# First stage of a fused attention and feed-forward layer: K and Q0 by halves of tokens, swapped on TensorE

## The reference

```
Q = x Wq^T + bq (32 heads of 16);  K, V = x Wk^T + bk, x Wv^T + bv (8 heads of 16)
Q, K = rope(Q, K)                  rope(a) = a * cos + rot_half(a) * sin
w = softmax(Q K^T / 4);  attn = w V;  y = LN(x + attn Wo^T + bo)
out = LN(y + ((silu(y Wg^T * gs) * (y Wu^T * us)) Wd^T) * ds)
```

## Time and profile before

| | us |
|---|---|
| median of 3 runs | 1176.72 |
| lowest and highest | 1174.79, 1180.6 |
| profiled execution, its own time | 1180.09 |
| its span in the trace | 1178.3 |
| mean granted TensorE clock | 0.961 of 2.4 GHz |

### The profile page before, as it was taken

The page is one execution under the profiler, slowest core; times in us unless marked ns, Lnnn a source line. Parts: engine busy times, 40 slices in busy tenths (PEclk is TensorE's granted clock), DMA queues, the critical chain, the costliest instruction groups (busy, mean ns, idle before and its releaser), DMA issues. The chain is left out here.

```text
span 1178.3 us, 14659 instructions
## 1 busy us (share of the span) xinstructions
PE 1091.8 (93%) x5634; PEld 543.7 (46%) x5634; DVE 786.6 (67%) x880; ACT 632.2 (54%) x1178; POOL 194.0 (16%) x158
## 2 busy tenths in 40 slices
PE   7799999999899999998999999999789899999995
PEld 4333333333333443333333333333336478888884
DVE  4488689996869768685569999999402345262534
ACT  1127688786668658682367878878453012222221
POOL 0290020000320011210003004980000100000002
PEclk9858999999899999999999999999799999999998
DMA  5862134127231413422015236511205020000000
GB/s 201 187 268 52 29 87 88 29 44 154 68 80 67 70 35 80 87 76 42 9 38 116 60 104 157 162 64 29 102 10 159 4 90 36 1 1 36 1 36 36
DMA packets 36139, 88.19 MB, mean 75 GB/s; under 512 B 12640, under 2 KB 12896, under 8 KB 33632
## 3 DMA queue, kind: packets, MB, share of 16 engines
q1 hardware_dynamic: 36064, 87.20, 28.3%
HBM read 49.43 MB, written 23.86 MB: 62 GB/s over the span
## 5 line engine op out<-in xcount | busy, mean ns | idle before, releaser
L342 DVE TENSOR_REDUCE nmx<-PSA 128x1 f32<-128x1024 f32 x512 | 600.0, 1216 | 125.4 <-PE PSA L331 125.2
L411 ACT ACTIVATE Bn<-PS 128x512 f32<-128x512 f32 x1024 | 530.2, 604 | 216.0 <-PE PS L405 215.7
L331 PE MATMUL PSA<-Kt,Qt 48*128 48x512 f32 x1024 | 411.9, 481 | 15.1 <-DVE nmx L342 9.6
L405 PE MATMUL PS<-Qt,Kt 50*128 50x512 f32 x1024 | 382.6, 455 | 40.0 <-ACT Bn L411 22.5
L405 PEld LDWEIGHTS PS<-Qt,Kt 50*128 50x128 f32 x1024 | 172.0, 188 | 342.9 <-ACT Bn L411 298.6
L424 PE MATMUL PV<-Bn 128*32 128x512 f32 x2048 | 280.1, 620 | 0.0
L331 PEld LDWEIGHTS PSA<-Kt,Qt 48*128 48x128 f32 x1024 | 174.3, 193 | 60.8 <-DVE nmx L342 41.4
L813 PE MATMUL PSA<-x1Th,wr 128*128 128x512 f32 x344 | 136.5, 397 | 0.5 <-DVE sg L833 0.5
L813 PE MATMUL PSA<-x1Tl,wr 128*128 128x512 f32 x344 | 135.2, 393 | 0.0
L833 DVE SCALAR_TENSOR_TENSOR sg<-PSA,us,sg 128x512 f32<-128x512 f32 x43 | 32.1, 748 | 137.4 <-ACT sg L824 137.2
L824 ACT ACTIVATE sg<-PSA,gs 128x512 f32<-128x512 f32 x43 | 29.5, 689 | 163.9 <-PE PSA L813 163.9
(11 more groups left out here) (84 smaller groups left out, 560.1 us busy)
## 6 DMA issues: line engine op xcount, KB each, us to landing
Qt<-pscr SPq DMA_DIRECT2D x96, 128.0 KB, 5.4
pscr<-A SPq DMA_DIRECT2D x20, 512.0 KB, 3.6
A<-in_wf SPq DMA_DIRECT2D x11, 768.0 KB, 7.0
wr<-A SPq DMA_DIRECT2D x33, 256.0 KB, 3.2
vscr<-Bn SPq DMA_DIRECT2D x32, 256.0 KB, 2.0
Kt<-pscr SPq DMA_DIRECT2D x96, 64.0 KB, 2.5
A<-A SPq DMA_DIRECT2D x20, 256.0 KB, 3.7
A<-in_xT SPq DMA_DIRECT2D x4, 1024.0 KB, 8.6
```

What stands on the lines that cost most here:

```text
L331: r = pe.do(lambda e, h=h, p=p: e.matmul(ps[:, h, :], Qt[i][p:p + NC_, g % 2, 128 * qt:128 * qt + 128], Kt[i][p:p + NC_, 512 * h:512 * h + ...
L342: r_mxs[hh, s] = dve.do(lambda e: e.tensor_reduce(nmx[:, hh % 2, c0:c0 + 1], ps, AX.XY, ALU.max, negate=True), c_rel[s])
L405: r = pe.do(lambda e: e.matmul(PS2[:, c % 3, :], Kt[i][rows, 128 * kt:128 * kt + 128], Qt[i][rows, g % 2, 512 * qh:512 * qh + 512], start= ...
L411: r_exp[c] = act.do(lambda e: e.activation(Pb[c % NP_], PS2[:, c % 3, :], ACT.Exp, scale=0.25), c_exp)
```

## The change

1. K and Q0 are made by halves of 512 tokens. The swap of the two 64-row halves is a matmul with a 128x128 permutation (`turn_pairs`), not two DMAs. POOL multiplies by cos, DVE by sin (straight from the PSUM bank), DVE adds. The parts go from SBUF straight into `Kt` and `Qt` of group 0 (`gather_k0`, `gather_q0`): 6 and 24 DMAs, of which ACT issues 2 and 6, and the first 16 maxima wait only for the first half of the queries. The way through DRAM stays for the later groups.
2. The products of V and Q1 are spread between the maxima: one V tile (four matmuls of 128 columns) or one Q1 matmul behind every second maximum. Their PSUM place is `PS2`. Q2 moves into unit (0,9), Q3 from (1,2) to (1,10). The copy of Q1 on ACT stands behind unit (0,2).
3. The loads of wo, bo, ds, gs, us go behind unit (0,0); x comes in eight pieces behind units (n,0) and (n,8) of groups 0 to 3. `add_bo(0)` goes behind (1,10), `add_bo(1)` behind (3,10).
4. Three float32 matmuls on constants stand ahead of K. ACT issues the loads of Wk, of the bias and of the permutation; the other loads have another order. `gather(2)` goes from (0,3) to (0,10).

```
+        def turn_pairs(i, h, bank, r_ev):
+            cols = slice(512 * h, 512 * h + 512)
+            raw, qrot, cos, sin = (x[:, cols] for x in (qraw[i], qrots[i], cosT, sinT))
+            pe.wait(r_ev, r_swap)
+            r_sw = pe.do(lambda e: e.matmul(bank, swap, raw, start=True, stop=True), c_swp)
+            pool.wait(r_ev, r_sw, r_cos)
+            r_c = pool.do(lambda e: e.tensor_tensor(raw, raw, cos, ALU.mult), c_cs)
+            dve.wait(r_sw, r_sin)
+            r_free = dve.do(lambda e: e.tensor_tensor(qrot, bank, sin, ALU.mult), c_rp)
+            dve.wait(r_free, r_c)
+            r = dve.do(lambda e: e.tensor_tensor(raw, raw, qrot, ALU.add), c_rp)
+            act.wait(r)
+            r_hi = act.do(lambda e: e.copy(qrot.bitcast(F32R), raw), c_hm)
+            dve.wait(r_hi)
+            r_lo = dve.do(lambda e: e.tensor_tensor(raw, raw, qrot, ALU.subtract), c_lo)
+            return r_hi, r_lo, r_free
...
+        def gather_q0(qh, r_hi, r_lo):
+            cols = slice(512 * qh, 512 * qh + 512)
+            for part, j, r in ((0, 0, r_hi), (0, 2, r_hi), (1, 1, r_lo)):
+                for g in range(4):
+                    q = act if qh == 0 and g >= 2 else sp
+                    q.wait(r)
+                    p = 64 * (g // 2) + 16 * j
+                    v = q.do(lambda e, p=p, g=g, part=part: e.dma_start(
+                        Qt[0][p:p + 16, g % 2, cols].bitcast(F32), (qrots, qraw)[part][1][g:128:8, cols]),
+                        c_rep0[qh], 16)
+            r_rep[0, qh] = v
...
-        first = [project(0, 4, True), project(0, 0, True)]
-        for k in range(3):
-            for g in first:
-                next(g, None)
-        gather(0)
-        r_vp[0] = values(0)
-        second, third = project(0, 1, False), project(0, 2, False, True)
-        next(second)
-        next(third)
-        gather(1)
-        load_late()
...
+        pe.wait(r_v1)
+        for _ in range(3):
+            pe.do(lambda e: e.matmul(PV[:, :], Vflat[:, 0:128], Vflat[:, 0:512], start=True, stop=True))
+        banks = [slot()[1], slot()[1]]
...
+        r_k = [fill(0, 0), fill(0, 1)]
+        r_part = [turn_pairs(0, h, PS2[:, h, :], r_k[h]) for h in range(2)]
+        r_q = [fill(1, 0)]
+        fill(1, 1, range(1))
+        gather_k0(*r_part[1][0:2])
+        r_part.append(turn_pairs(1, 0, PS2[:, 2, :], r_q[0]))
+        gather_q0(0, *r_part[2][0:2])
+        r_q.append(fill(1, 1, range(1, KT)))
+        r_part.append(turn_pairs(1, 1, PV[:, :], r_q[1]))
+        r_idle.append(r_part[3][2])
+        vals, second = values(0, True), project(0, 1, True)
+        next(vals)
+        gather_q0(1, *r_part[3][0:2])
...
+        fine = itertools.chain(vals, second)
+        for k in range(8):
+            advance(4)
+            next(fine, None)
+        for k in range(LEAD):
+            advance(4)
+            next(fine, None)
+        for _ in range(16 - 1 - 8 - LEAD):
+            next(fine, None)
+        put(0, 2, lambda: next(second, None))
+        put(0, 4, lambda: next(second, None))
+        put(0, 0, lambda: load_late("wo", "bo", "ds", "gs", "us"))
+        for part in range(4):
+            put(part // 2, 8 * (part % 2), lambda part=part: load_x(0, part))
+            put(2 + part // 2, 8 * (part % 2), lambda part=part: load_x(1, part))
+        put(1, 10, lambda: add_bo(0))
+        put(3, 10, lambda: add_bo(1))
+        spread(project(0, 2), 0, 9, (6, 2))
+        spread(project(0, 3), 1, 10, (6, 2))
```

More of the change, by code:

```diff
@@ L1 @@
+import itertools
 from contextlib import ExitStack
@@ L228, in post_ln_layer, with product, project @@
         r_idle = []
-        def project(b, m, fast, idle=False):
+        def product(ps, b, m, h, k, c):
+            pe.wait(r_wqk[m], r_xT[b][h])
+            last_xT[b] = pe.do(lambda e: e.matmul(ps, wqk[:, m, k, :], xT[:, h, k, :], start=(k == 0), stop=(k == KT - 1)),
+                               c)
+            return last_xT[b]
+        def project(b, m, idle=False):
             s, ps = (None, PS2[:, 0:2, :]) if idle else slot()
-            pe.wait(r_wqk[m])
+            if idle:
+                pe.wait(r_idle[-1])
             for h in range(2):
-                pe.wait(r_xT[b][h])
                 for k in range(KT):
[L237 to L240, removed]
-            last_xT[b] = r
+                    r = product(ps[:, h, :], b, m, h, k, c_fill if (h, k) == (1, KT - 1) else None)
+                    if idle and (h, k) != (1, KT - 1):
+                        yield
             i = qn[0] % 2
@@ L280, in values @@
                         start=(k == 0), stop=(k == KT - 1)), c_fill if last else None)
+                if idle and t < 7:
+                    yield
             last_xT[b] = r
@@ L287, in values @@
                     bv[:, :].rearrange("p (o v c) -> p o v c", o=1, v=NKV).to_broadcast([128, 4, NKV, HD]),
-                    ALU.add), c_v if h == 0 else c_rel[s])
-            return c_rel[s].now()
+                    ALU.add), c_v if idle or h == 0 else c_rel[s])
+            r_vp[b] = v
+            if idle:
+                r_idle.append(v)
+            yield
+        r_vp = {}
         c_mr = [count(f"c_mr{i}") for i in range(3)]
@@ L327, in maxima @@
             s, ps = slot()
-            pe.wait(r_rep[n])
+            pe.wait(r_rep[n, qt // 4])
             for h in range(2):
@@ L564, in put, with fill @@
             background.setdefault((n, w), []).append(f)
+        pe.wait(r_v1)
+        for _ in range(3):
+            pe.do(lambda e: e.matmul(PV[:, :], Vflat[:, 0:128], Vflat[:, 0:512], start=True, stop=True))
+        banks = [slot()[1], slot()[1]]
+        def fill(i, h, ks=range(KT)):
+            m = (4, 0)[i]
+            for k in ks:
+                r = product(banks[i][:, h, :], 0, m, h, k, c_fill if k == KT - 1 else None)
+            if ks[-1] < KT - 1:
+                return None
+            act.wait(r, r_bqk)
+            return act.do(lambda e: e.activation(qraw[i][:, 512 * h:512 * h + 512], banks[i][:, h, :], ACT.Identity,
+                                                 bias=bqk[:, m:m + 1]), c_ev if h == 0 else c_rel[i])
+        qn[0] = 2
+        r_k = [fill(0, 0), fill(0, 1)]
[11 more added lines that the diff above has]
+        gather_q0(1, *r_part[3][0:2])
+        for i, m in enumerate((4, 0)):
+            sp.wait(r_part[2 * i + 1][1])
+            write_parts(0, m, i)
+            free_raw[i] += (c_rep0[0].now(), c_rep0[1].now())
+        gather(1)
         stream = [(n, qt, g) for n in range(NG) for qh in range(2) for qt in range(4 * qh, 4 * qh + 4)
@@ L581, in advance @@
                 next(halves, None)
-        for k in range(16):
-            if k == 4:
-                next(second, None)
-            if k == 8:
-                next(third, None)
-            if k == 13:
-                next(second, None)
-            advance(2)
-        advance(4 * LEAD)
-        next(third, None)
-        add_bo(0)
-        add_bo(1)
-        spread(project(0, 3, False), 1, 2, (6, 2))
+        fine = itertools.chain(vals, second)
[17 more added lines that the diff above has]
+        spread(project(0, 3), 1, 10, (6, 2))
         def load_b1():
@@ L1076 @@
         "ident": np.eye(128, dtype=np.float32),
+        "swap": np.roll(np.eye(128, dtype=np.float32), 64, 0),
     }
```

84 lines of the change are left out of this document (53 added, 31 removed).

## The result

| | before | changed |
|---|---|---|
| median, us | 1175.76 (4 runs, 1173.67 to 1180.6) | 1190.07 (4 runs, 1188.18 to 1196.95) |
| ratio | | 1.0126, 95% interval 1.0074 to 1.0179 |
| profiled span, us | 1178.3 | 1189.3 |
| mean granted clock | 0.961 | 0.964 |

The medians differ by 14.3 us, the forecast said 8.2; 1190.07 lies inside the range of 1171 to 1199. The ratios leave out runs more than 1.5% above the fastest of the same kernel, so a ratio can differ from that of two medians.

The account below looks back on a forecast made before the run. TensorE, busy 93% of the span, was taken as the bound, so an added matmul costs its own time unless PE waits there. Terms -6.0 + 7.5 + 6.2 + 0.5 = +8.2 us gave 1184.9 from the median; range 1171 to 1199.

Parts of the forecast that it names:

- The first reduction: VectorE's first maxima reduction moves from 49.39 to about 34.9 us; sign: a start at 33 to 36 us.
- From there to the end of Q1: First reduction to Q1's product, 34.9 to 71 us: 12 pairs 29.4, V's evacuation 1.3, Q1 matmuls 3.4, low clock 2.
- From there to unit 3: Q1's product to unit 3's V matmuls takes 19.5 us, to 90.5; ACT's copy of Q1 waits 3 to 5.
- My price for having no such wait: At Q1's copy on ACT: with the rotation early enough, unit 3 would come 7 us better.
- Q2's block: Q2's projection, moved from the gap ahead of the maxima into unit 9, costs +7.5 us.
- The split: Split of group 1's maxima behind unit 11 waits for Q2's POOL rotation: +6.2 us with low clock, bounds 0 and 6.2.
- `add_bo(1)`: Behind unit 58 it meets the split behind unit 59: one or two instructions of 1.2 us, partly hidden, +0.5 us.
- The copies of Q2 and the sum on ACT: These copies on ACT come closer together: cost nothing, bound 1 us.
- The sum: First stage -6.0, Q2's block +7.5, split +6.2, `add_bo(1)` +0.5: whole kernel +8.2 us, chance 0.42.
- A: Rival, first stage: the clock holds as PE's gap shrinks under 2 us; about -1 us, 1175.7 us, chance 0.20.
- B: Rival: the split behind unit 11 misses POOL; +2.0 us, 1178.7 us, chance 0.22.
- C: Rival: low clock lasts through V and Q1; 12 pairs cost 17 us instead of 2; +24 us, 1201, chance 0.16.

Follow-up runs that it names:

- E5: Changed kernel with five more constant matmuls between Q0's last products and the swap of its second half; ratio 1.0064 to before, median 1189.67 us against 1180.35.
- E1: Changed kernel with Q1's copy on ScalarE behind unit (0,5) instead of (0,2), its write behind (0,7); ratio 1.0142 to before, median 1190.63 us.
- E3: Changed kernel with Q1's copy behind unit (0,5), its write behind (0,7), and Q2's products in unit (0,10); ratio 1.0112 to before, median 1189.31 us.
- E4: Kernel before with one part alone: Q2's products in unit (0,9) instead of ahead of the maxima; ratio 1.0134, median 1189.20 us against 1175.43.
- E2: Changed kernel with Q2's products in unit (0,10) instead of (0,9); ratio 1.0098 to before, median 1193.19 us over 10 runs.
- E9: Kernel before with Q2's products alone moved from the gap ahead of the maxima into unit (0,10); ratio 1.0124, median 13.2 us above before.
- E12: The changed kernel measured once more, unchanged, over 9 runs; ratio 1.0105 to before.
- E7: Changed kernel with five V tiles ahead of the last swap, three behind; Q1 and Q2 between maxima, Q1's copy ahead of scores; 1175.28 us against 1180.35, ratio 0.9961.

## Why the prediction was right, and where its sizes were off

**The first reduction: forecast 34.9, measured 38.13**, outside the 33 to 36 us that were named as its sign. The method was right, the low-clock steps and the issues were under-priced. The issues on ACT cost 0.66 us each, not the 0.46 read from SP: +1.2. It isn't a matter of the queue: four of K's DMAs held SP for 2.77 us, 0.69 each, so the row taken, six reads from DRAM, was no measure for copies from SBUF to SBUF. The swap at the low clock took 2.07 instead of 0.89 (+1.2), and the V tile behind it, at that clock too, held the maxima, for which the reduction waited 0.46 us. The prediction let the clock fall only in the phase after the gap and priced none of the gap's own successors with it. The blocked add was as forecast: 1.67 us instead of 0.69, and the sin product at 16.08, which reads PSUM, took 0.69 beside POOL. By the rule of the Trainium skill (SBUF — State Buffer, "SBUF: two separate sides") it should be so, and the trace agrees.

**From there to the end of Q1: forecast 36.1 us, measured 36.7** (38.13 to 74.87). Right in sum, and partly by luck: the clock was low for about 14 us (59 to 72.7) where I had put 4, and by E5, where it held, that cost 3.9 us and not 2. Most of the pairs ran at the high clock and cost nothing.

**From there to unit 3: forecast 19.5, measured 18.6** (74.87 to 93.50). POOL ended the rotation 12.7 us after Q1's product, exactly as forecast. ACT came to the copy later, since the units ahead of it ran slowly too, so it waited 2.64 us, less than the 3 to 5 named as the sign. My price for having no such wait, 7 us, failed: E1 puts it at 2.7 and E3 at 1.8. Together the first stage gave -3.0 and not -6.0 at unit 3; nearly all of the miss is the late first reduction.

**Q2's block: forecast +7.5, measured +7.4**, here and in E4, and 7.5 to 7.6 in E2 and E9. **The split: forecast +6.2, measured +6.5** in the trace, with the releaser, the place and the low clock as forecast. The cast began 5.57 us after Q2's bias (forecast 5.6) and POOL 4.68 us after it (forecast 4.43). It returned in every kernel that has Q2 in unit 9, between 5.3 and 9.3 us. The prediction's reason, two SBUF operands, is too narrow for its own rows: the cast has one input, and beside POOL it took 1.51 us instead of 0.17, as it had in the earlier trace rows. The forecast took its price from such a meeting, so it didn't suffer. (Where the prediction says 6.3 for this term, its own sum has 6.2.) **`add_bo(1)`: forecast +0.5**; at unit 60 the differences show no step. The copies of Q2 and the sum on ACT, priced at nothing with a bound of 1, cost nothing that the marks show in unit 9. With Q2 in unit 10 they cost 0.9 us in E9; the 3.3 us of E2 and E3 began with the late write behind `gather(2)`, for which the prediction had no term.

**The sum**: -3.0 + 7.4 + 6.5 = +10.9, and the spans differ by 11.0. That these agree so closely is partly luck, since E12's difference moved between +11.8 and +8.3 behind unit 64. The medians differ by 14.3, and by 13.6 in E12's series, where the forecast had 8.2. The marks account for 2.7 of the 6.1 us that it was too low, nearly all from the late first reduction. The other 3.4 is no term of the sum: the profiled run of before lies 3.4 to 4.3 us above its median, the changed kernel's near its own, and no mark shows where the unprofiled runs differ.

**The rivals.** A (the clock holds) is out: the gap was 5.09 us, and even where E5 held the clock through the maxima it fell in the first units. B (the split misses POOL) didn't happen in any kernel with Q2 in unit 9. C (the low clock lasts) happened in E1's and E3's executions, between 30 and 78 us. From the first reduction to the first exponential E1 took 44.6 us with the clock low all along and E5 34.6 with it high, so the 12 pairs cost 10.0 and not the 17 that I had put on them: a pair took 3.41 us at the low clock (six from 37.50 to 57.96), not 4.0.

## What to carry to other kernels

Work taken out of an idle gap and put into a stream in which TensorE is busy 93% of the time costs its full length; look first whether the place it leaves was free, and E4 is the test to make before all others. A moved block brings its followers along: ask where its products on GpSimd meet VectorE's next cast or two-operand instruction, and where its writes stand in SP's queue ahead of something urgent. When two queues share the issue of a batch of DMAs, emptying one only lengthens the other.

## What the runs showed of the hardware that I had not expected

- A DMA issue of 16 partitions x 512 held ACT's queue for 0.66 us (3.98 us for 6), one of 16 x 1024 SP's for 0.69 (2.77 for 4).
- A cast with one SBUF input took 1.51 us instead of 0.17 while POOL multiplied, so not only instructions with two operands are held.
- TensorE's clock stood at 0.50 from 60 to 72 us while PE was busy 12.00 of 12 us, and in E1 from 40 to 58 us with 18.00 of 18. Being busy did not by itself bring it back.
- The same program up to the first exponential gave 76.60 and 76.90 us in two executions; with an edit that acts only later it gave 82.11 (E1) and 82.41 (E3).
- Over 75 runs of the kernel before the time falls by 9.7 us per 0.01 of the mean granted clock. A comparison of two kernels that differ by 1% has to look at it, but can't correct by it: E7's gain of 5 us goes with a clock of 0.971, at which it lies 6.2 us above that line.
